# Three grouped attention layers as one rolling pipeline of equal tiles, with the narrow products joined

## What is computed

```
xn = rmsnorm(x, norm_w)
q = (xn @ wq).reshape(B, T, 16, 32)
k = (cond @ wk).reshape(B, S, 4, 32)          # 4 key heads: each serves 4 query heads
v = (cond @ wv).reshape(B, S, 4, 32)
scores = einsum('btgrd,bsgd->bgrts', q in groups, k) / sqrt(32)
attn = softmax(scores)
out = einsum('bgrts,bsgd->btgrd', attn, v)
x = x + out @ wo
```

## Time and profile before

| | us |
|---|---|
| median of 3 runs | 4371.97 |
| lowest and highest | 4371.32, 4375.28 |
| the profiled execution | 4374.92 |
| its span, first to last instruction | 4373.1 |
| contexts (first stretch) | 0 to 1004 |
| first layer | 1004 to 2148 |
| start of the grouped layers | 2148 to 2241 |
| grouped layers | 2241 to 4373 |

### The profile page before, as it was taken

How to read it: one execution, slowest core, us unless ns; L and a number is a source line. 1 busy time by engine, 2 the same in 40 slices (tenths; PEclk the granted TensorE clock), 3 DMA queues, 4 the chain that set the end, 5 groups by cost and what they waited for, 6 DMA issues and landing times.

```text
span 4373.1 us, 62922 instructions
## 1 busy us (share of the span) xinstructions
PE 4149.7 (95%) x19566; PEld 2627.3 (60%) x19566; DVE 2592.1 (59%) x3521; ACT 2034.7 (47%) x2569; POOL 1907.0 (44%) x985
## 2 busy tenths in 40 slices
PE   9999999997999999999799999989999999999999
PEld 7888888884555665556445555545555554555555
DVE  3112300015556555665587777787777778777777
ACT  2111211113444444444256666566665666566665
POOL 0000000004556555555355655555565655656555
PEclk9999999998999999999899999999999999999999
DMA  5333522225445444444422223322332223322333
GB/s 184 131 132 130 167 81 82 91 89 144 121 127 134 125 120 130 129 128 132 122 76 71 76 86 88 95 77 76 86 90 84 76 81 95 91 79 76 86 88 103
DMA packets 320880, 457.02 MB, mean 105 GB/s; under 512 B 46168, under 2 KB 118872, under 8 KB 320824
## 3 DMA queue, kind: packets, MB, share of 16 engines
q1 hardware_dynamic: 320824, 456.27, 36.4%
HBM read 222.77 MB, written 102.77 MB: 74 GB/s over the span
## 4 chain that ended last, share of the span: by engine, by line
PE 36%; DVE 5%; ACT 5%; issue 4%; SPq 0%; ACTq 0%; DVEq 0%; POOL 0%; DMA 0%
PE a_ps L1229 7%; PE a_ps L1189 7%; PE a_ps L1256 6%; PE a_ps L1213 6%; PE a_ps L1171 6%; ACT a_probs L948 4%; DVE x_lo L1042 2%; PE a_ps L1240 2%; PE a_ps L1245 1%; DVE a_max_cols L1036 1%; PE a_ps L1196 1%; PE a_ps L1159 1%; DVE a_stage L1052 0%; DVE a_qf L1026 0%; DVE a_results L1074 0%
## 5 line engine op out<-in xcount | busy, mean ns | idle before, releaser
L1036 DVE TENSOR_REDUCE a_max_cols<-a_ps 128x1 f32<-128x512 f32 x2086 | 1361.6, 683 | 625.5 <-PE a_ps L1189 621.9
L948 ACT ACTIVATE a_probs<-a_ps 128x1024 f32<-128x1024 f32 x1024 | 1012.0, 1026 | 629.4 <-PE a_ps L1213 620.7
L1213 PE MATMUL a_ps<-a_q_ops,a_k_ops 128*128 128x512 f32 x2560 | 792.1, 411 | 60.9 <-ACT a_probs L948 49.6
L1189 PE MATMUL a_ps<-a_k_ops,a_q_ops 96*128 96x512 f32 x2086 | 815.9, 429 | 33.0 <-DVE a_qf L1026 11.3
L826 POOL TENSOR_TENSOR a_sums<-a_probs 128x1024 f32<-128x1024 f32 x256 | 606.3, 2384 | 426.7 <-ACT a_probs L948 426.7
L826 POOL TENSOR_TENSOR a_sums<-a_sums,a_probs 128x1024 f32<-128x1024 f32 x320 | 764.9, 2401 | 20.7 <-POOL a_sums L826 20.3
L1229 PE MATMUL a_ps<-a_probs,a_v 128*32 128x512 f32 (+1 forms) x4096 | 646.0, 606 | 34.1 <-ACT a_probs L948 32.3
L1189 PEld LDWEIGHTS a_ps<-a_k_ops,a_q_ops 96*128 96x128 f32 x2086 | 387.6, 191 | 432.3 <-DVE a_max_cols L1036 265.0
L1213 PEld LDWEIGHTS a_ps<-a_q_ops,a_k_ops 128*128 128x128 f32 x2560 | 450.5, 190 | 315.7 <-ACT a_probs L948 222.0
L1052 DVE RECIPROCAL a_stage<-a_stage 128x128 f32<-128x128 f32 x640 | 556.5, 916 | 119.9 <-ACT a_stage L924 119.9
L803 POOL MEMSET a_ident<- 128x128 f32 x2 | 0.4, 206 | 993.3 <-issue 993.3
(11 more groups left out here) (89 smaller groups left out, 5321.9 us busy)
## 6 DMA issues: line engine op xcount, KB each, us to landing
a_k_ops<-k_scratch SPq DMA_DIRECT2D x201, 256.0 KB, 3.9
a_q_ops<-a_qn_hi SPq DMA_DIRECT2D x792, 64.0 KB, 2.0
k_scratch<-cp_out SPq DMA_DIRECT2D x88, 512.0 KB, 2.8
a_q_ops<-a_qn_hi SPq DMA_DIRECT2D x268, 128.0 KB, 2.3
cp_raw<-in_ctx_t SPq DMA_DIRECT2D x64, 512.0 KB, 4.1
x_raw<-out_t SPq DMA_DIRECT2D x26, 1024.0 KB, 5.5
a_q_ops<-a_qn_lo SPq DMA_DIRECT2D x396, 64.0 KB, 2.0
a_x_res<-out_t SPq DMA_DIRECT2D x96, 256.0 KB, 3.2
```

What stands on the lines that cost most here:

```text
L948: act.activation(probs[:, s], ps[:, 2 * (s % 2):2 * (s % 2) + 2, :], ACT.Exp)\
L1036: dve.tensor_reduce(max_cols[:, t % 2, col:col + 1], bank(max_bank(p)), AX.X, ALU.max, negate=True).then_inc(reduced, 1)
L1189: pe.matmul(bank(max_bank(p)), q_ops[0:SHIFT, s, h, PASS - 1, q * P:(q + 1) * P], k_ops[0:SHIFT, s, k_head(h), PASS - 1, :], start=True, s ...
L1213: last = pe.matmul(bank(2 * (n % 2) + j), k_ops[:, s, k_head(h), p, kt * P:(kt + 1) * P], q_ops[:, s, h, p, :], start=(p == 0), stop=(p == ...
```

## The change

`attention_layers(... "a1" ...)` is replaced by a new function `grouped_layers`. The same matmuls are made on the same shapes. What differs:

- **Equal tiles.** Each tile has 16 maxima, one q projection and one quarter of an output projection, which belongs to the batch before: in tile t stands block (t - 5) modulo 4, five tiles late (`LAG`). Four pieces (`project_out`, tiles 0 to 3) stand in different places of the tile. Nothing is left for the end of the batch. `a_hi` and `a_lo` become double.
- **Joined narrow groups.** Output groups 0 and 1 stand together in the tile; groups 2 and 3 stand in the tile behind, directly ahead of both denominator groups.
- **PSUM.** Maxima use banks 4 and 5 alone. The transposition goes to bank 5 (`TURNB`), the denominators, the q projection, the output projection and the sum of squares share bank 7 (`FB`).
- **Shift** is halved: two copies behind exponential 6, two behind exponential 7.
- `normalise` moves from VectorE to GpSimd, for which ScalarE copies the outputs out of PSUM (`take_outputs`, one more 128x512 copy a tile).
- VectorE spreads reciprocals, the parts of the mean square's inversion, and x's split (four pieces of 128x512 instead of one of 128x2048) among its reductions.
- The loop has two batches an iteration; the first and the last two batches are written out, and work of batches that don't exist is left out there. The weights of the output projection lie in the upper half of the shared `wq` buffers, and values are double buffered.

The core of the diff, in the order of the engines' streams:

```diff
+    LEAD = M + 6
+    LAG = T + 1
+    OUTB, FB, TURNB = 6, 7, 5
+    MAXB = (4, 5, 4, 5, 4, 5, 4, 5, 4, 5, 4, 5, 4, 4, 4, 5)
...
+        @block.scalar
...
+            def batch(it, par):
+                for t in range(T):
+                    exponential(it, t, 0)
+                    if there(it, t - 2):
+                        round_output(*at(it, t - 2), par if t >= 2 else 1 - par)
+                    if there(it, t - 1):
+                        take_outputs(*at(it, t - 1))
+                        take_denominators(*at(it, t - 1))
+                    exponential(it, t, 1)
...
+                    exponential(it, t, 2)
+                    exponential(it, t, 3)
+                    if there(it, t + AHEAD):
+                        round_q(*at(it, t + AHEAD))
...
+                    exponential(it, t, 6)
+                    if there(it, t + 1):
+                        shift(*at(it, t + 1), 0)
+                    exponential(it, t, 7)
+                    if there(it, t + 1):
+                        shift(*at(it, t + 1), 1)
...
+        @block.vector
...
+            def batch(it, par):
...
+                    maximum(it, t, 2)
+                    reciprocal(*at(it, t - 1), 0)
+                    maximum(it, t, 3)
+                    maximum(it, t, 4)
+                    reciprocal(*at(it, t - 1), 1)
+                    maximum(it, t, 5)
+                    if there(it, t + AHEAD):
+                        take_q(*at(it, t + AHEAD))
+                    maximum(it, t, 6)
...
+                    if t == T - 1 and there(it, 2 * T):
+                        mean_square(it + 2, FB)
+                    maximum(it, t, 7)
+                    maximum(it, t, 8)
+                    reciprocal(*at(it, t - 1), 2)
+                    maximum(it, t, 9)
+                    maximum(it, t, 10)
+                    reciprocal(*at(it, t - 1), 3)
+                    maximum(it, t, 11)
...
+                    if t == 0 and there(it, T):
+                        split_x(it + 1, 0)
+                    maximum(it, t, 12)
...
+                    if t == 0 and there(it, T):
+                        split_x(it + 1, 1)
+                    maximum(it, t, 13)
...
+                    if t == 0 and there(it, T):
+                        split_x(it + 1, 2)
...
+                    maximum(it, t, 14)
+                    if there(it, t - LAG):
+                        add_result(it, t)
+                    maximum(it, t, 15)
...
+        @block.tensor
...
+            def maximum(it, t, i):
+                t_m, n = max_target(it, t, i)
+                if there(it, t_m):
+                    no = tile_no(it, t) * M + LEAD + i
+                    if i == 15:
+                        pe.wait_ge(shifted, 2 * (tile_no(it, t) + 2))
+                    else:
+                        pe.wait_ge(reduced, no if i in (13, 14) else no - 1)
+                    one_maximum(*at(it, t_m), n, MAXB[i])
...
+            def scores(it, t, n):
+                g, s, kt, hp = tile_no(it, t), t % RING, n // (H // 2), n % (H // 2)
+                if n < 2:
+                    pe.wait_ge(shifted, 2 * g + 1 + n)
+                wait(pe, exped, g * NS + n - 1)
...
+            def batch(it, par):
+                for t in range(T):
+                    scores(it, t, 0)
+                    maximum(it, t, 0)
+                    outputs(*at(it, t - 1), KT - 2, par if t > 0 else 1 - par)
+                    outputs(*at(it, t - 1), KT - 1, par if t > 0 else 1 - par)
+                    denominators(*at(it, t - 1))
+                    maximum(it, t, 1)
+                    scores(it, t, 1)
+                    maximum(it, t, 2)
+                    maximum(it, t, 3)
+                    project_q(*at(it, t + AHEAD), range(2))
+                    scores(it, t, 2)
+                    maximum(it, t, 4)
+                    project_q(*at(it, t + AHEAD), range(2, 3))
+                    maximum(it, t, 5)
+                    project_q(*at(it, t + AHEAD), range(3, 4))
+                    scores(it, t, 3)
+                    maximum(it, t, 6)
...
+                    if t == T - 1 and there(it, 2 * T):
+                        pe.wait_ge(q_taken, tile_no(it, t) + AHEAD + 1)
+                        sum_squares(it + 2, FB)
+                    maximum(it, t, 7)
+                    scores(it, t, 4)
+                    maximum(it, t, 8)
+                    project_out(it, t, par, 0)
+                    maximum(it, t, 9)
+                    project_out(it, t, par, 1)
+                    scores(it, t, 5)
+                    maximum(it, t, 10)
+                    outputs(it, t, 0, par)
+                    outputs(it, t, 1, par)
+                    maximum(it, t, 11)
+                    scores(it, t, 6)
+                    maximum(it, t, 12)
+                    project_out(it, t, par, 2)
+                    turn(*at(it, t + 1))
+                    maximum(it, t, 13)
+                    scores(it, t, 7)
+                    maximum(it, t, 14)
+                    project_out(it, t, par, 3)
+                    maximum(it, t, 15)
```

560 lines of the change are left out of this document (558 added, 2 removed).

## The result

| kernel | time, median (range), us | span, us | TensorE busy, us | mean clock |
|---|---|---|---|---|
| before | 4373.6 (4371.3 to 4377.4) | 4373.1 | 4149.7 | 0.988 |
| after | 4583.1 (4574.4 to 4590.1) | 4588.3 | 4193.5 | 0.959 |

The change makes the kernel slower by 4.8%: ratio 1.0477, 95% interval 1.0456 to 1.0499. The forecast was 4426 us, its range ended at 4490. The direction was right, the size was not: about 54 us were forecast, and 210 came.

What follows compares the result with a forecast made beforehand. TensorE was taken as the bound in the grouped layers. A batch of 91.8 us against 88.7 gave +70 over 23 batches; start and end terms brought this to +54, so 4426 us, range 4343 to 4490.

Steps and rivals of the forecast that it cites:

- The hold: Maximum 15 waits for ScalarE's copies, starting 4.06 us behind the transposition; TensorE stands still up to 1.95 us a tile.
- The tile: A steady tile of the new kernel takes 22.5 us, against 22.2 in the kernel before.
- The wait at maximum 8: TensorE waits 0.6 us there for VectorE's reductions, reciprocal and taking of q.
- The 0.35 at maximum 3: Maximum 3 waits 0.35 us until maximum 1, in the same bank, is reduced.
- The fourth tile: In a batch's fourth tile the sum of squares waits for q and takes time: +0.85 us.
- The first tile: VectorE splits x in pieces between maxima 11 to 14 beside GpSimd's sums: +0.9 us, between 0.1 and 3.
- the +3: First tile if three x pieces each wait out a whole GpSimd operation: +3 us, the time 48 us above the forecast.
- rival C: TensorE's clock falls after waits: 4474 us if every fourth hold brings a fall, 4618 if every one does; 17%.
- C's own sign: Matmuls of 0.63 us in most tiles of the new profile would show the clock rival.
- The splits of weights: At a grouped layer's start they cost nothing, bounded by 3 us either way for each of three layers.
- the prediction's own signs of being wrong: Copies done before the projection's last piece, a batch under 88 us, or a TensorE wait put at nothing appearing.
- The switches: Into narrow products and back costs TensorE 0.32 us; two left a tile, so 5.8 us a batch becomes 2.6.

Runs made afterwards that it cites:

- all three edits: Kernel after with four copies ahead of exponential 7, x's pieces split in the second tile, next scores ahead of maximum 15: 4351.4 us, ratio 0.9949.
- The three edits: Each alone against the kernel after: copies ahead of exponential 7, 4473.3 us; x's pieces in the second tile, 4543.4; next scores ahead of maximum 15, 4502.3.
- the fastest kernels: Kernel after with copies, pieces and scores moved, maxima spread and all batches written out: 4253.0 us; the same with maximum 14 behind the last output projection piece: 4252.7.

## Why the prediction was right or wrong

- **The hold, right.** It was named, placed, and sized: 4.14 for 4.06 us behind the transposition. Taking it away gave 110 us, more than any other edit. The profile's 95 us of stillness stand where "near 150" was forecast, because VectorE's waits at maxima 13 and 14 cover part of it and not every tile has one.
- **The tile, right in sum, less so in its parts:** 22.42 for 22.5. The wait at maximum 8 was 0.21 for 0.6. The 0.35 at maximum 3 is not seen while the hold is there; with all three edits it is 0.53 in the tile that was read.
- **The fourth tile:** 1.12 for 0.85. Right.
- **The first tile, near in sum by luck.** The step read one subtraction of four pieces at 3.05 us and derived 0.6 to 1.7 for a piece. That mean hides two cases: 0.68 us where GpSimd is idle, and up to 2.96 where it is not. The Trainium skill, which the prediction cites, page "SBUF — State Buffer", section "Who interferes with whom", is right on the block: each of the 47 delayed pieces ended 0.55 us behind a GpSimd operation. But the +3 that the prediction drew from the rule doesn't come at full clock. The tile shown came to 3.11, of which 1.6 is the clock, and moving the pieces took 22 us of idle time away, 1.0 a batch, for 0.9 in the sum. The delay lies in part where the hold for the copies would have stood.
- **The clock, wrong, and the largest miss.** The sum had it at zero, and rival C had 17% with "every fourth hold" as its main case. In 64 of 93 stretches the clock was below full, which is C's own sign. C was the right mechanism, and the error was to keep it apart as a rival: it is no other way in which the case could go but a price on every wait in the sum. The three edits show that price in busy time: 41, 16 and 52 us.
- **The jump, missing.** The description of the change and the prediction both had the loop's new shape in view, and no step gave it a price. It is 3.2 to 3.8 us a jump, 42 us in all with what follows from it.
- **The splits of weights, wrong.** The step put them at nothing, bounded by 3 us for each of three layers. They hold TensorE for 9 us at each, 27 us, because VectorE's four operations and ScalarE's rounding ahead of them stand in front of the first output product. No experiment moved them: 25.7 us are left with all three edits, and 29 in the fastest kernels. A wait on TensorE that was put at nothing is one of the prediction's own signs of being wrong.
- **The switches, right in price and wrong in meaning.** Joined groups save their 0.32 us, but the maxima that stood between them then have nothing over their reductions. The sum saw that for maxima 3 and 8. What the joined groups are worth alone is less than nothing in the kernel before.

The pitch accounts for it. Forecast 91.8, measured 99.7, 7.9 apart: 0.1 for the first tile at full clock, 0.3 for the fourth, -0.3 for four tiles of 22.42, 1.5 for the jump (32.3 us in 21 batches) and 1.3 for the splits of weights (27.0), which leaves 5.0 for the clock. The last number is a remainder, and holds whatever else I have not told apart. The granted clock bears it out: in these 21 batches it is 0.94, which withholds 6.0 us a batch, and TensorE is busy for 88% of the time, 5.3. So does the busy time: 100 us between after and the kernel with all three edits, 4.4 us for each of 23 batches.

The other side of the difference was off too. The sum took 88.70 us, the pitch of one batch, for that of the kernel before; its mean over 22 batches, from the mean square at 2297.28 to that at 4276.71, is 90.0. So the change costs 9.7 us a batch where the sum had 3.05, and 6.7 x 23 = 153 us, against the 4590.1 - 4428.6 = 161 by which the profiled run missed. The 8 us that are left are the start and the end together, for which the sum had -16; what their terms came to one by one is not known.

**Where the change's gain is.** The plan is sound once its waits are moved: written out, with its copies, pieces and scores moved and its maxima spread, it takes 4253 us, 2.8% less than before (0.9723, interval 0.9707 to 0.9740). TensorE's stretch from 2241 on then has the clock of before:

```profile
2241.00:4180.00 1939.00, 1854.92 (x9876) 1087.40 (x9880) 1541.87 (x2227) 1312.02 (x1618) 1308.09 (x709) 0.99 0.33 88
```

**What stays open.** Why the holds lower the clock in one tile and not in another. Behind the hold of 1.32 us at 3277.15 the 16 joined products take 1.92 us. Behind one of the same length at 3371.25 they take 3.12:

```profile
3371.25 0.50 PE L2017 MATMUL a_ps<-a_k_ops,a_q_ops 96*128 96x512 f32 x1 [1.32 <-ACT a_q_ops L1769]
...
3372.79 3.12 PE L2063 MATMUL a_ps<-a_probs,a_v 128*32 128x512 f32 x16
```

So the length of the last wait alone doesn't decide. Open is also why the kernel before has no gap at its own loop's jump: a body of one batch may stay at hand, for which its few fetched packets speak, but no run had one batch a pass in the new kernel. And what the splits of weights would give back if they stood elsewhere, some 29 us by the waits, was not run.

## What to carry to other kernels

- Price a wait on TensorE with the clock that it costs: here holds of 75 us in all took another 41 with them, and useless matmuls put into a hold made the kernel faster. Then check what a regular order puts behind a wait; moving one group of scores ahead of it was worth 81 us.
- Work on VectorE with two operands in SBUF belongs where GpSimd is idle or where nobody waits for VectorE. Its cost depends on what it meets, so a mean says little: look for the shortest and the longest row.
- Work that comes once a layer is easily put at nothing; look for its few long waits (here three of 9 us) and not only at the steady tile.
- When a loop's body grows, look for rows without a releaser at its first instruction; joining small work into groups is only worth its switches if what stood between it finds other cover.

## What the runs showed of the hardware

- A jump back in a loop of two batches holds TensorE for 3.2 to 3.8 us in the kernel after, and no releaser is named; written out, the same kernel has no such gap.
- 0.93 us of additional wide matmuls a tile, in a hold, raised busy time by 35 us where 84 were added, since more of the others ran at the higher clock.
- A 128x512 subtraction on VectorE takes 0.68 us, or until 0.55 us behind the end of the GpSimd operation that it met (47 of 92, 2.96 us at worst).
- The same hold of 1.32 us was followed by full clock in one tile and by the lower level in another.
- In a row of five maxima the last four start 0.60 us apart, the pace of VectorE's reductions.
